# Products of two constants, into an unread PSUM bank, during TensorE's waits in routing, ahead of attention, among the last heads and in the last feed-forward

## What is computed

```
x = x + mamba4(reaction_diffusion(x, zX, zY, zR))      # 4 scan blocks, 16 states, 256 channels
x = x + moe(cond_ffn(x, ids))                          # top 2 of 8 experts, 128 -> 512 -> 128
x = x + attention(prompt_pool(x, types))               # latent kv of rank 128, 16 heads of 64, causal
x = x + bitlinear_ffn(subject_linear(x, ids))          # levels of +-127, gelu, 128 -> 512 -> 128
```

## Time and profile before

| | us |
|---|---|
| median of 3 runs | 1406.49 |
| lowest and highest | 1405.2, 1406.69 |
| profiled execution | 1419.78 |
| its span | 1417.9 |
| TensorE busy | 1274.1 (90%) |
| VectorE busy | 1161.4 (82%) |
| GpSimd busy | 1116.0 (79%) |
| ScalarE busy | 1010.2 (71%) |
| mean granted clock of TensorE | 0.961 |

### The profile page before, as it was taken

How to read it: one execution, slowest core, us unless ns; L and a number is a source line. 1 busy time by engine, 2 the same in 40 slices (tenths; PEclk the granted TensorE clock), 3 DMA queues, 4 the chain that set the end, 5 groups by cost and what they waited for, 6 DMA issues and landing times.

```text
span 1417.9 us, 19876 instructions
## 1 busy us (share of the span) xinstructions
PE 1274.1 (90%) x5370; PEld 710.9 (50%) x5379; DVE 1161.4 (82%) x1686; ACT 1010.2 (71%) x2389; POOL 1116.0 (79%) x684
## 2 busy tenths in 40 slices
PE   6698998989989999999999999599949999999994
PEld 2243343334334344334334456599935666676663
DVE  7899999999999999999999988755635566566564
ACT  4778878878877877887887886333318777787772
POOL 7889999999999999999999994144347776675661
PEclk9699999999999999999999999799969999999997
DMA  4644264154344434525415444223120000000000
GB/s 142 267 194 186 98 251 188 68 237 179 119 198 179 161 144 186 208 103 238 187 69 230 180 133 154 67 60 105 42 60 16 12 24 13 12 19 17 9 9 8
DMA packets 48978, 169.26 MB, mean 119 GB/s; under 512 B 15704, under 2 KB 33436, under 8 KB 40716
## 3 DMA queue, kind: packets, MB, share of 16 engines
q1 hardware_dynamic: 46636, 163.78, 30.2%
q0 software_dynamic: 2272, 4.66, 1.5%
HBM read 160.75 MB, written 7.67 MB: 119 GB/s over the span
## 4 chain that ended last, share of the span: by engine, by line
PE 46%; DVE 23%; ACT 14%; issue 12%; DMA 2%; POOL 1%; DVEq 0%; ACTq 0%; SPq 0%; POOLq 0%
DVE h L1233 13%; ACT banks L1198 9%; PE banks L1268 7%; DVE h L1214 5%; PE banks L403 5%; PE banks L728 4%; PE banks L789 3%; PE banks L766 3%; PE banks L412 2%; PE banks L670 2%; PE banks L685 2%; PE banks L705 2%; PE banks L804 2%; PE banks L1285 2%; PE banks L1119 2%
## 5 line engine op out<-in xcount | busy, mean ns | idle before, releaser
L1239 POOL TENSOR_TENSOR h<-h,Cb 128x1024 f32<-128x1024 f32 (+1 forms) x180 | 584.8, 3276 | 25.9 <-DVE h L1233 15.5
L1233 DVE TENSOR_TENSOR_SCAN h<-banks,h 128x1024 f32<-128x1024 f32 x256 | 573.8, 2276 | 16.4 <-ACT banks L1198 16.1
L1198 ACT ACTIVATE banks<-dt,A_cur 128x255 f32<-128x255 f32 x1024 | 422.1, 461 | 86.9 <-DVE h L1233 84.7
L1268 PE MATMUL banks<-h,ident 128*128 128x512 f32 x1024 | 468.8, 597 | 4.4 <-POOL h L1239 2.6
L1268 PEld LDWEIGHTS banks<-h,ident 128*128 128x128 f32 x1024 | 189.9, 190 | 246.5 <-issue 224.4
L1214 DVE TENSOR_TENSOR h<-Bb,banks 128x1024 f32<-128x1024 f32 (+1 forms) x131 | 204.5, 1566 | 3.6 <-ACT banks L1182 3.6
L1220 POOL TENSOR_TENSOR h<-Bb,u 128x1024 f32<-128x1024 f32 x80 | 188.6, 2369 | 0.1
L758 POOL TENSOR_SCALAR h<-h 128x128 f32<-128x128 f32 (+1 forms) x128 | 95.6, 764 | 69.7 <-DVE h L751 69.6
L758 POOL TENSOR_SCALAR Cb<-Cb,h 128x128 f32<-128x128 f32 (+1 forms) x128 | 102.8, 821 | 32.5 <-DVE h L751 32.4
L1093 PE MATMUL banks<-xn,wF 128*128 128x512 f32 x256 | 115.3, 602 | 7.3 <-ACT xn L1085 7.3
L1093 PEld LDWEIGHTS banks<-xn,wF 128*128 128x128 f32 x256 | 48.9, 192 | 72.2 <-issue 61.6
(11 more groups left out here) (295 smaller groups left out, 2047.2 us busy)
## 6 DMA issues: line engine op xcount, KB each, us to landing
Bb<-scrX SPq DMA_DIRECT2D x32, 2048.0 KB, 8.1
Cb<-scrX SPq DMA_DIRECT2D x32, 2048.0 KB, 9.7
h<-in_L_ffn_w SPq DMA_DIRECT2D x2, 2048.0 KB, 8.7
by_expert<-Cb SPq DMA_DIRECT2D x39, 64.0 KB, 1.5
h<-in_conv_w SPq DMA_DIRECT2D x4, 512.0 KB, 3.9
scr<-h SPq DMA_DIRECT2D x3, 640.0 KB, 15.3
wF<-scr SPq DMA_DIRECT2D x3, 512.0 KB
dt<-in_pmask SPq DMA_DIRECT2D x4, 257.0 KB
```

The costliest lines, as they stand in the source:

```text
L1198: m = e.activation(ps_dA[c % 2][:, g, half, 1:S], dts[q][:, half, i * S + 1:(i + 1) * S], ACT.Exp, scale=A_cur[q][:, s:s + 1])
L1233: e.tensor_tensor_scan(chunk(i, c), ps_dA_flat[c % 2], chunk(i, c), 0.0, ALU.mult, ALU.add).then_inc(sem("scan"), 1)
L1239: e.tensor_tensor(h[i][:, rows(cs), :, :], h[i][:, rows(cs), :, :], both(Cb[i], cs), ALU.mult).then_inc(sem("hC"), len(cs))
L1268: m = e.matmul(bank(5), ident[:], h_flat[i][:, s * HALVES * S:(s + 1) * HALVES * S], start=(s == 0), stop=(s == NS - 1))
```

## The change

A helper `turn_over(e, k, n)` issues n products of the constants `center_w` and `ident` (both 128 x 128, fp32) into the first 128 columns of bank k. They signal nothing and nothing reads the result. Words in TensorE's orders call it: `spin:8` between `list:0` and `ranks:2` and `spin:28` behind `xt:3`, the last word of routing (bank 0, after a wait for all eight features evicted); `heat:40` ahead of `x2t` and `hold:18` ahead of `pturn`, for batch 0 alone (bank 2, no wait); `warm` for the last batch alone (bank 5, after a wait for its four evicted values): `warm:5` behind `turn:12` and `warm:3` behind `values:5` in the pass k = 7, and `warm:l2` behind `values:l7`, `warm:l8` behind `fc` and `warm:l23` behind `fu:1` in the pass k = 8. Nothing else is changed, on no engine.

```diff
--- before.py
+++ after.py
@@ -565,6 +565,19 @@
                     e.scalar_tensor_tensor(out=xt[:, j, :], in0=picked[b % 3][:, k, t, :], scalar=w[:, j:j + 1],
                                            in1=xt[:, j, :], op0=ALU.mult, op1=ALU.add).then_inc(sem("mo_acc"), 1)
 
+        def turn_over(e, k, n):
+            for _ in range(n):
+                e.matmul(bank(k, P), center_w[:], ident[:], start=True, stop=True)
+
+        def pe_heat(e, b, n):
+            if b == 0:
+                turn_over(e, 2, n)
+
+        def pe_warm(e, b, n):
+            if b == B - 1:
+                e.wait_ge(sem("v_sb"), 4 * B)
+                turn_over(e, 5, n)
+
         def pe_x2t(e, b):
             e.wait_ge(sem("mo_acc"), 4 * b + 4)
             wait(e, sem("x2T"), 3 * b)
@@ -925,7 +938,7 @@
 
         PIECES = dict(
             gp=dict(gather=(4, gp_gather), mask=(2, gp_mask), norm=(0, gp_norm)),
-            pe=dict(x2t=(2, pe_x2t), at=(2, pe_at), S=(2, pe_S), pturn=(1, pe_pturn), pool=(1, pe_pool), lat=(1, pe_lat), q=(1, pe_q), k=(1, pe_k), v=(1, pe_v),
+            pe=dict(heat=(2, pe_heat), hold=(1, pe_heat), warm=(0, pe_warm), x2t=(2, pe_x2t), at=(2, pe_at), S=(2, pe_S), pturn=(1, pe_pturn), pool=(1, pe_pool), lat=(1, pe_lat), q=(1, pe_q), k=(1, pe_k), v=(1, pe_v),
                     V=(0, pe_v), score=(0, pe_score), turn=(0, pe_turn), values=(0, pe_values),
                     o2=(-1, pe_o2), fx=(-1, pe_fx), fc=(-1, pe_fc), fqturn=(-1, pe_fqturn),
                     fu=(-1, pe_fu), fq2turn=(-1, pe_fq2turn), fd=(-1, pe_fd)),
@@ -1487,6 +1500,10 @@
                 m = e.matmul(home[:, d * NE:n * NE], ones_w, tot16[:, lo * NE:(hi - d) * NE], start=False, stop=(d == n - 1))
             m.then_inc(sem("rank"), 1)
 
+        def pe_spin(e, n):
+            e.wait_ge(sem("rT"), B)
+            turn_over(e, 0, n)
+
         def pe_total(e, _):
             e.wait_ge(sem("run"), len(GROUPS))
             e.wait_ge(sem("lg_sb"), len(GROUPS))
@@ -1649,7 +1666,7 @@
             pe_out(e, LAST, LQ)
 
         FINAL_PE = dict(list=pe_list, lnc=pe_lnc, lnt=pe_lnt, up=pe_up, down=pe_down, logits=pe_logits, rows=pe_rows, ranks=pe_ranks,
-                        total=pe_total, xt=pe_xt, outlast=pe_out_last)
+                        total=pe_total, xt=pe_xt, outlast=pe_out_last, spin=pe_spin)
         FINAL_ACT = dict(sq=act_lnsq, rs=act_lnrs, sc=act_lnsc, gelu=act_gelu, rT=act_rT, rows=act_rows,
                          xt=act_xt, shift=act_shift, ones=act_ones)
         FINAL_DVE = dict(fin=dve_final, lnsc=dve_lnsc, Clast=dve_C_last, gatelast=dve_gate_last, reslast=dve_res_last)
@@ -1921,9 +1938,9 @@
 ATT_GP = """
 gather:l1 gather:0 norm:4 norm:5 norm:6 norm:7 norm:n0 mask norm:n1 norm:n2 norm:n3"""
 ATT_PE = """
-score:3 v:l1 turn:0 V:2 turn:1 values:l7 score:4 turn:2 V:3 o2 turn:3 values:0 pturn fx score:5 pool turn:4 values:1
-fc score:6 turn:5 lat turn:6 values:2 q:0 turn:7 score:7 k:0 fqturn q:1 fu:0 turn:8 values:3 fu:1 turn:9 score:n0
-x2t turn:10 q:2 turn:11 k:1 values:4 turn:12 score:n1 q:3 turn:13 at k:2 values:5 turn:14 score:n2 fq2turn k:3
+score:3 v:l1 turn:0 V:2 turn:1 values:l7 warm:l2 score:4 turn:2 V:3 o2 turn:3 values:0 hold:18 pturn fx score:5 pool turn:4 values:1
+fc score:6 turn:5 lat turn:6 values:2 q:0 turn:7 score:7 k:0 warm:l8 fqturn q:1 fu:0 turn:8 values:3 fu:1 warm:l23 turn:9 score:n0
+heat:40 x2t turn:10 q:2 turn:11 k:1 values:4 turn:12 warm:5 score:n1 q:3 turn:13 at k:2 values:5 warm:3 turn:14 score:n2 fq2turn k:3
 turn:15 S v:0 values:6 fd"""
 ATT_ACT = """
 prob:6 pexp turned:1 V:3 prob:7 pturned yturned:0 turned:3 prob:8 fx prob:9 yturned:1 prob:10 turned:5 prob:11 lat
@@ -1959,8 +1976,8 @@
 PE_LAST = """
 sum:l6 sum:l7 out up:0 sum:a0 up:1 sum:a1 down:0 down:1 sum:a2 sum:a3 sum:a4 up:2 sum:a5 up:3 sum:a6 down:2 sum:a7
 down:3 lnc:2 sum:b0 sum:b1 sum:b2 sum:b3 logits:0 sum:b4 lnt:2 sum:b5 sum:b6 rows:0 sum:b7 up:4 ranks:0 up:5 outlast
-rows:1 lnc:3 down:4 down:5 lnt:3 logits:1 rows:2 up:6 up:7 ranks:1 down:6 down:7 logits:2 list:0 ranks:2 total:0
-rows:3 xt:0 list:1 list:2 xt:1 xt:2 list:3 xt:3"""
+rows:1 lnc:3 down:4 down:5 lnt:3 logits:1 rows:2 up:6 up:7 ranks:1 down:6 down:7 logits:2 list:0 spin:8 ranks:2 total:0
+rows:3 xt:0 list:1 list:2 xt:1 xt:2 list:3 xt:3 spin:28"""
 ACT_NEXT = """
 xn dA:a2 dA:a3 silus xm:0 exps dA:a4 shift:0 dA:a5 dA:a6 res dA:a7 ucopy:b dA:b0 silus xm:1 shift:1 zs:0 zs:1 exps
 xd dA:b1 dA:b2 dA:b3 sp_abs sp_exp sp_ln dA:b4 dA:b5 sq:0 dA:b6 rs:0 dA:b7 ucopy:n sc:0 dA:n0 sq:1 rs:1 sc:1 dA:n1"""
```

## The result

| | before, us | after, us |
|---|---|---|
| median | 1406.67 (5 runs) | 1400.22 (5 runs) |
| lowest, highest | 1405.2, 1407.98 | 1399.83, 1401.28 |
| profiled execution, its span | 1419.78, 1417.9 | 1401.28, 1399.5 |
| mean granted clock of TensorE | 0.961 | 0.984 |

The ratio is 0.9956, with a 95% interval from 0.9942 to 0.9971: 6.4 us faster. The forecast was 1399.5 us and a gain of 7.0 us.

The account below looks back on a forecast made before the run. TensorE was taken to bound stretches where it finishes last at half clock, having waited shortly before. Terms 1.5 + 3.6 + 1.0 + 0.9 = 7.0 us off the 1406.5 us median gave 1399.5 us, range 1394.5 to 1404.5 us.

Parts of the forecast that it names:

- Routing: Blocks of 8 and 28: the first two expert tiles run at full clock; 1.5 us taken, at most 2.3 us.
- the start of attention: Blocks of 40 and 18: pooling through q:1 run warm, 4.35 us, less 0.7 us overrun; 3.6 us taken.
- the last heads: Blocks of 5, 3 and 2 in the last batch: last transposes and values products warm; 1.0 us, bounds 2.0 and -0.8.
- all of it arrives: Rival for the whole change: every bound at its better end, 9.8 us gained, 1396.5 us; chance 0.20.
- the good sign: Ahead of attention: pooling transposes come no later than 5.5 us after the score row.
- the bad one: Ahead of attention: pooling transposes come over 6 us after the score row, showing the forecast wrong.
- The other signs: First tile 1.8 us, clock 1.00 at 918 us, q:0 and k:0 0.86 us, late transposes 0.5 and 0.6 us.
- Last feed-forward: Blocks of 8 and 23: transposes and down products after the last gelu warm; 0.9 us, bounds 1.1 and -3.9 us.
- The fourth rival, no effect: At attention's start the gain is given back at the next gather or load: 1406 us; chance 0.08.
- The rival that ends slower: Blocks of 18, 28 and 23 stay at low clock and overrun by 10.6 us together: 1417 us; chance 0.07.

Follow-up runs that it names:

- e5: The changed kernel with each filler product replaced by two fp32 transposes of the same constant: 1400.76 us, ratio 0.9954 to the kernel before.
- e2: The kernel before with only routing's blocks of 8 and 28 fillers: 1403.48 us, against 1406.68 us for the kernel before on that chip.
- e1: The kernel before, without any edit, profiled once more: 1406.16 us.
- e3: The kernel before with only the blocks of 40 and 18 ahead of attention: 1404.61 us, against 1406.68 us for the kernel before on that chip.
- e6: The changed kernel with 46 fillers in place of 23 in the last wait: 1405.05 us, ratio 0.9986 to the kernel before.
- e7: The changed kernel with the gap before attention filled (46 for 40, 26 for 18, two twos between): 1399.93 us, ratio 0.9953 to the kernel before.
- e8: The changed kernel with 23, 11 and 22 more fillers at the opening of the scan layers: 1402.1 us, ratio 0.9967 to the kernel before.
- e9: The changed kernel without the blocks of 5, 3 and 2: 1415.85 us, against 1414.52 us for the kernel before on that third chip.
- e11: The changed kernel without the block of 40: 1411.59 us, against 1414.52 us for the kernel before on that third chip.

## Why the prediction was right, and where it was not

**The total.** 7.0 us were forecast and 6.4 us measured, and the mechanism is the one forecast: the fillers keep the clock up, and the work behind them takes about half its time. That the sum came so close is partly luck. Routing was put 0.8 us too low, the start of attention some 0.4 us too high, and the last heads perhaps 1.0 us too high; these errors cancel.

**Routing, 1.5 us forecast, too low.** From the first tile's transpose to the product with `mean_w` just ahead of the last down product of the expert loop, the five profiles without these blocks have 110.0 to 111.7 us, mean 111.1; the nine others 108.5 to 109.0 us, mean 108.7. That is 2.3 us, the upper bound of the step, to the tenth. I had taken off for fillers that end too early or too late. They did so without harm: the block of 28 took 8.0 us in the changed kernel, low clock at its start included, and 6.3 us in e5, where it left 1.96 us, and the first tile was at full clock in both. e2 measured 2.8 to 3.2 us.

**Start of attention, 3.6 us forecast, a little too high, and right in mechanism.** From the pooling transposes to the first score it went from 10.5 us to 6.2 us, 4.3 us, against the profile that I read, and the sum had 4.35 us. In e1 and e2 it was 10.0 and 9.9 us: the clock had come up earlier in the stretch, so that the gain against the mean of the five profiles without the blocks (10.3 us) is 4.1 us. The overrun of the 18, taken as 0.7 us, was 1.1 us in the changed kernel, 0.6 us in e3, 1.3 us in e5 and none in e6 and e7. Over the whole stretch from the first transposes of batch 0 the gain is 3.2 us in the changed kernel (19.2 against 16.0 us), 3.0 us in e3, 3.3 us in e5, and 3.6 us in e6. That the clock falls between the 40 and the 18 and returns within the 18 was right: 1040 to 1047 us. That the faster first transposes gain nothing because of GpSimd's queue was right nearly to the end: in the changed kernel VectorE's row came 0.2 to 0.4 us sooner after them than without the blocks, in e3, e6 and e7 0.2 to 0.5 us later.

Two things in the forecast do not hold together here. It gives this step an upper bound of 4.9 us, for which it has no terms; its terms end at 4.35 us, and the rival "all of it arrives" uses 4.4 us (1406.5 less 9.8 us is 1396.7, not 1396.5 us). And it named as a sign of being wrong that the pooling transposes come over 6 us after the score row, and as a sign of being right that they come within 5.5 us. They came 6.0 us after it in the changed kernel and 6.6 us in e3, so the good sign failed and the bad one was reached. It was a poor sign: in e7, where nothing was held up, they came 6.4 us after it, because the row ends earlier when it is warm and VectorE's row does not. The other signs came true: 1.79 us for the first tile, clock 1.00 at 918 us, q:0 and k:0 in rows of 1.03 us that follow each other in 0.86 us, 0.55 and 0.62 us for the two transposes.

**Last heads, 1.0 us forecast.** 0.8 us in the mean over the profiles, between 0 and 2.0 us, for the reason given: the fall is no fixed feature. In the three profiles of the first set, the only ones without these blocks in which attention has no waits of 1.7 to 2.0 us, it is 0, so the 6.4 us may hold nothing of it. No run takes out these blocks alone on such a chip.

**Last feed-forward, 0.9 us forecast.** 0.8 to 0.9 us by the profiles, with and without (19.1 or 19.2 against 18.2 to 18.4 us). By the medians no run resolves it.

**The profiled execution against the median.** I saw no part of the 13.3 us in the stretches touched and took the gain off the median. That was right in effect, and the reason incomplete: the waits at the values products, which I used in the earlier trace rows as evidence of how unsteady the clock is, are themselves 9 us that the median of those runs does not have. Half of the evidence for "no fixed feature" came from a state of affairs that the measured runs did not share.

**What the prediction did not see.** It has no case for a gain that depends on the chip. The fourth rival, no effect, came closest with its 1406 us, and its place was right, the start of attention, but its mechanism (given back at the next gather or load) was not: on the third chip the pooling is late at once, behind a late hand-over. On that chip alone the forecast of "faster" would have been wrong. The rival that ends slower, fillers at the low clock throughout, did not occur; its price, an overrun paid in full, did (e6).

## What to carry to other kernels

Where TensorE waits and then carries the path, filling the wait with products that nobody reads buys back up to half of the work behind it; size the block so that it ends just before the work at the price of the clock it will really have, and check that the wait ends with TensorE's own work due, since a filled wait ahead of work with slack (e8) can move the low stretch onto something else. Price each block by the work behind it alone, and read a second profile before trusting a stall that one profile shows. Measure on more than one chip: here the same kernel gained 6.4 us on one and nothing on another.

## What the runs showed of the hardware that I had not expected

- Transposes in fp32 raise and hold the clock as products do: 0.112 us a record, 6.28 us for 56, the clock up inside a block of 36 of them, ratio 0.9954 against 0.9956 with products (e5).
- The clock fell behind waits of 1.75 and 0.84 us with work between them in e9 (0.51 from 1386 to 1393 us). In e3, a single wait of 2.59 us left the transposes directly behind it at the price of full speed (0.44 us).
- The same code ahead of attention saw the clock low for 3.4 us in one execution (e6) and for 6.8 us in another (the changed kernel).
- One chip, in the one set run on it, shows late hand-overs: the reader starts on a result of TensorE about 1.1 us after its recorded end at three places of every profile, 1.3 us after it at one more in e11, and over 5 us after it at one place of two kernels. In attention, no profile of the other two chips has such a place; the first profile of before, whose chip is not known, has the three.
